# Wv's preparation merged into the block of LN1 and V, with the x rows loaded ahead of Wv and the weight maxima of four tiles put behind their rows

## The reference

```python
# x: (1, 2048, 1024) float32; 16 heads of 64; FFN of 2752 with NF4 weights in blocks of 64
def reference(x, Wq, Wk, Wv, Wo, gate, up, down):      # each FFN weight: codes and scales
    h = layernorm(x)
    q, k, v = rotary(h @ Wq), rotary(h @ Wk), h @ Wv
    attn = softmax(causal(q @ k.T) / 8) @ v
    x = x + layernorm(attn @ Wo)
    h = layernorm(x)
    y = (silu(h @ dequant(gate).T) * (h @ dequant(up).T)) @ dequant(down).T
    return x + layernorm(y)
```

## Time and profile before

| | |
|---|---|
| median of three runs | 3296.17 us |
| the profiled execution | 3296.03 us, span 3294.2 us |
| TensorE matmul busy | 2897.0 us (88%) |
| VectorE busy | 2390.9 us (73%) |
| ScalarE busy | 2022.5 us (61%) |
| GpSimd busy | 121.6 us (4%) |
| TensorE's granted clock, mean | 0.964 of full |
| first projection matmul of V starts | 47.70 us after the span's start |
| first matmul of the Q and K projection | 242.61 us |

### The profile page before, as it was taken

One profiled execution on the slowest core, in us unless ns is written; L12 is line 12 of the kernel. 1 busy time (PEld: TensorE's weight loads), 2 busy tenths in 40 slices (PEclk: granted clock), 3 DMA queues, 4 the chain that ended last, 5 costly groups with the idle time before them and its releaser, 6 DMA issues. The chain is left out here.

```text
span 3294.2 us, 58839 instructions
## 1 busy us (share of the span) xinstructions
PE 2897.0 (88%) x17856; PEld 1547.4 (47%) x17856; DVE 2390.9 (73%) x4289; ACT 2022.5 (61%) x4003; POOL 121.6 (4%) x397
## 2 busy tenths in 40 slices
PE   4989999688888888985883699999999999999996
PEld 2534444466666666663441244444444444444442
DVE  6535555688888888884556787787777777777767
ACT  1114443688888888882214767676676676676742
POOL 0000000000000000000002000000000000000002
PEclk9999999899999999997996899999999999999998
DMA  4322222201010101102112111111111111111124
GB/s 164 116 77 58 76 76 64 72 22 40 22 41 22 40 22 35 27 5 86 64 70 69 53 52 49 50 52 52 46 52 49 50 52 45 53 46 52 52 71 153
DMA packets 77773, 188.88 MB, mean 57 GB/s; under 512 B 12304, under 2 KB 12688, under 8 KB 77200
## 3 DMA queue, kind: packets, MB, share of 16 engines
q1 hardware_dynamic: 77456, 185.13, 17.7%
HBM read 151.52 MB, written 33.55 MB: 56 GB/s over the span
## 5 line engine op out<-in xcount | busy, mean ns | idle before, releaser
L1234 PE MATMUL gp<-region,wgu 128*128 128x512 f16 x4224 | 931.3, 383 | 89.3 <-DVE wgu L1392 89.3
L1271 ACT ACTIVATE line<-code,offsets 128x512 f32<-128x512 f32 x1056 | 697.2, 713 | 111.3 <-DVE below L1370 45.7
L1234 PEld LDWEIGHTS gp<-region,wgu 128*128 128x128 f16 x4224 | 416.0, 99 | 600.9 <-issue 110.9
L786 ACT ACTIVATE probs<-logits,nbias,coef 128x512 f32<-128x512 f32 (+3 forms) x640 | 461.0, 720 | 100.4 <-POOL nbias L719 86.4
L1247 PE MATMUL yp<-wd,inter 128*128 128x512 f16 x2112 | 463.9, 380 | 24.5 <-DVE wd L1392 17.4
L835 DVE SCALAR_TENSOR_TENSOR pt_pair<-tp,pt_pair 128x512 f16<-128x512 f32 (+3 forms) x640 | 385.8, 603 | 76.2 <-ACT pt_pair L795 72.4
L736 PE MATMUL logits<-k_sb,q_sb 128*128 128x512 f16 (+3 forms) x1280 | 347.3, 354 | 104.6 <-ACT probs L786 61.2
L819 DVE TENSOR_REDUCE mx<-logits 128x1 f32<-128x512 f32 (+3 forms) x640 | 383.9, 600 | 33.7 <-PE logits L736 33.1
L795 ACT ACTIVATE pt_pair<-tp 128x512 f16<-128x512 f32 (+3 forms) x640 | 343.4, 537 | 25.2 <-PE tp L749 21.0
L749 PE MATMUL tp<-ident,probs 128*128 128x128 f32 x2176 | 349.2, 276 | 4.3 <-DVE pt_pair L835 2.7
L548 PE MATMUL pq<-region,wt_pair 128*128 128x512 f16 x1536 | 333.4, 380 | 14.9 <-DVE wt_pair L599 14.9
(11 more groups left out here) (107 smaller groups left out, 2823.0 us busy)
## 6 DMA issues: line engine op xcount, KB each, us to landing
qk_pairs<-r_pair SPq DMA_DIRECT2D x128, 128.0 KB, 2.1
k_sb<-qk_pairs SPq DMA_DIRECT2D x64, 256.0 KB, 5.4
cst<-in_gate_codes SPq DMA_DIRECT2D x44, 256.0 KB, 2.6
sst<-in_gate_scales SPq DMA_DIRECT2D x88, 128.0 KB, 2.9
cst<-in_up_codes SPq DMA_DIRECT2D x44, 256.0 KB, 2.7
sst<-in_up_scales SPq DMA_DIRECT2D x88, 128.0 KB, 3.1
cst<-in_down_codes SPq DMA_DIRECT2D x44, 256.0 KB, 2.7
sst<-in_down_scales SPq DMA_DIRECT2D x88, 128.0 KB, 3.0
```

Of the source, the lines that this page charges most:

```text
L786: a.activation(probs[:, g0 % P_RING, 0:w * P], sp_[:, g0 % S_RING, 0:w * P], ACT.Exp, bias=nbias[:, m:m + 1], scale=col(coef, 0), accum_ou ...
L1234: mm = pe.matmul(gp[:, e % 2, m, :], wgu[:, par, m, a, col0:col0 + P], xnT[:, b, k, tok], start=(k == 0 and a == b), stop=(k == KT - 1 and ...
L1271: a.activation(line[:, k % 4, :], code7[:, :], ACT.Identity, scale=slope, bias=offsets[:, k:k + 1]).then_inc(s_L.sem, 1)
```

## The change

- The first block is gone. Its work stands in the block of LN1 and V, in the same lists as the x tiles.
- SyncE's order: x tile 0, four Wv tiles, x tile 1, four Wv tiles, weights of tiles 0 and 1, `flat`, x tiles 2 and 3, weights of tiles 2 and 3; from tile 4 on rows and weights in turn as before.
- VectorE's order: rows of tile 0, four Wv maxima, rows of tile 1 and low half of tile 0, four Wv maxima, all-reduce and factor of Wv alone, eight low halves of Wv, tiles 2 and 3 of rows with `lo` and `v_lo` as in the loop but without weight maxima; then in one piece the weight maxima of tiles 0 to 3, the clearing of `sums` and the maxima of `flat`; then the loop, with weight maxima inside `rows` again.
- The first projection waits for each low half of Wv by itself (`s_wvlo`) in its first 24 matmuls.
- GpSimd: constants, inverse roots of tiles 0 and 1, the all-reduce of Wv's maximum, then the other roots.
- The last all-reduce and the factors at the block's end take seven columns for three, and three coefficient products moved there from the first block.

```diff
@@ -188,7 +188,7 @@
         mask_f32 = sb("mask_f32", [P, P], F32, c04)
         mask_bf = sb("mask_bf", [P, P], BF16, c04)
         sums = sb("sums", [P, ST, HEADS, SC], F32, c04)
-        Q_, K_, O_, V_, G_, U_, D_ = range(7)
+        Q_, K_, O_, G_, U_, D_, V_ = range(7)
 
         def col(t, n):
             return t[:, n:n + 1]
@@ -217,79 +217,6 @@
 
         c01 = ctx.enter_context(ExitStack())
         wv_pair = sb("wv_pair", [P, 2, KT, E], F16, c01)
-        ...
-        c0.close()
-
         def layernorm_stats(v, chain, parts, st, variance):
 
             for n, part in enumerate(parts):
@@ -309,6 +236,8 @@
 
 
         c1 = ctx.enter_context(ExitStack())
+        flat = sb("flat", [P, 3, I * E // BLOCK // P], F32, c1)
+        vmax = sb("vmax", [P, KT], F32, c1)
         xt = sb("xt", [P, 2, E], F32, c1)
         ht = sb("ht", [P, 2, E], F32, c1)
         wst = sb("wst", [P, 2, 3, CH], F32, c1)
@@ -318,6 +247,15 @@
         vp = ps("vp", [P, 2, 2, CH], F32, c1)
         d_x = loads("d_x", 2)
         d_ws = loads("d_ws", 2, 3)
+        d_wv = loads("d_wv", KT)
+        d_flat = loads("d_flat", 1, 3)
...
         s_c1 = sem("s_c1")
         s_h = signal("s_h", 2)
         s_wm = signal("s_wm", 2)
@@ -341,17 +279,34 @@
 
             @block.sync
             def _(sp):
-                def step(i, it, u):
+                def rows(i, u):
                     sp.wait_ge(s_h.sem, s_h.room(i))
                     sp.dma_start(xt[:, u, :], x_tiles[bass.ds(i, 1)].rearrange("a p e -> p (a e)")
                                  ).then_inc(d_x.sems[u], 16)
+
+                def weights(i, u):
                     sp.wait_ge(s_wm.sem, s_wm.room(i))
                     for m in range(3):
                         sp.dma_start(wst[:, u, m, :], w_parts[m][bass.ds(i, 1)].rearrange("a p e -> p (a e)")
                                      ).then_inc(d_ws.sems[u], 16)
-                with sp.Fori(0, ST // 2) as it:
+                wv_v = wv.rearrange("(k p) n -> p k n", p=P)
+                rows(0, 0)
+                for k in range(KT):
+                    sp.dma_start(wv_f32[:, k, :], wv_v[:, k, :]).then_inc(d_wv.sems[k], 16)
+                    if k == 3:
+                        rows(1, 1)
+                for u in range(2):
+                    weights(u, u)
+                for m in range(3):
+                    sp.dma_start(flat[:, m, :], scales_flat[m]).then_inc(d_flat.sems[0], 16)
+                for u in range(2):
+                    rows(2 + u, u)
+                for u in range(2):
+                    weights(2 + u, u)
+                with sp.Fori(2, ST // 2) as it:
                     for u in range(2):
-                        step(it * 2 + u, it, u)
+                        rows(it * 2 + u, u)
+                        weights(it * 2 + u, u)
 
             @block.tensor
             def _(pe):
@@ -364,19 +319,25 @@
                         mm = pe.transpose(tp[:, u, k, :], ht[:, u, k * P:(k + 1) * P], ident[:, :])
                     mm.then_inc(s_T1.sem, 1)
 
-                def project(i, u):
+                def project(i, u, first=False):
                     pe.wait_ge(s_tlo.sem, s_tlo.done(i))
                     pe.wait_ge(s_vlo.sem, s_vlo.room(i))
                     for n in range(2):
                         for k in range(KT):
+                            if first and n == 0:
+                                pe.wait_ge(s_wvlo.sem, s_wvlo.done(k))
                             for a, b in ((0, 0), (0, 1), (1, 0)):
                                 mm = pe.matmul(vp[:, u, n, :], hT[:, a, k, bass.ds(i * P, P)],
                                                wv_pair[:, b, k, n * CH:(n + 1) * CH],
                                                start=(k == 0 and a == b), stop=(k == KT - 1 and a == 1))
                     mm.then_inc(s_V.sem, 1)
 
+                pe.wait_ge(s_id.sem, s_id.done(4))
                 transposes(0, 0)
-                with pe.Fori(0, ST // 2 - 1) as it:
+                for u in range(2):
+                    transposes(u + 1, 1 - u)
+                    project(u, u, u == 0)
+                with pe.Fori(1, ST // 2 - 1) as it:
                     for u in range(2):
                         transposes(it * 2 + u + 1, 1 - u)
                         project(it * 2 + u, u)
@@ -397,6 +358,10 @@
                                  scale=QKV_DOWN).then_inc(s_vhi.sem, 1)
 
                 hi(0, 0)
+                a.wait_ge(s_facv.sem, s_facv.done(0))
+                for k in range(KT):
+                    a.activation(wv_pair[:, 0, k, :], wv_f32[:, k, :], ACT.Copy,
+                                 scale=col(wfac, V_)).then_inc(s_wvhi.sem, 1)
                 with a.Fori(0, ST // 2 - 1) as it:
                     for u in range(2):
                         hi(it * 2 + u + 1, 1 - u)
@@ -410,16 +375,20 @@
                 for s in (s_h, s_wm, s_tlo, s_vlo):
                     v.sem_inc(s.sem, s.credit)
 
-                def rows(i, it, u):
-
-                    chain = Count(s_c1, i * CHAIN1)
-                    v.wait_ge(d_x.sems[u], d_x.done(it))
-                    layernorm_stats(v, chain, (xt[:, u, 0:CH], xt[:, u, CH:E]), st1[:, u, :], s_var1)
+                def weights(i, it, u):
                     v.wait_ge(d_ws.sems[u], d_ws.done(it))
                     for m in range(3):
                         mx = v.tensor_reduce(wmax[:, m, bass.ds(i, 1)], wst[:, u, m, :], AX_X, ALU.max,
                                              apply_absolute_value=True)
                     mx.then_inc(s_wm.sem, 1)
+
+                def rows(i, it, u, between=None):
+
+                    chain = Count(s_c1, i * CHAIN1)
+                    v.wait_ge(d_x.sems[u], d_x.done(it))
+                    layernorm_stats(v, chain, (xt[:, u, 0:CH], xt[:, u, CH:E]), st1[:, u, :], s_var1)
+                    if between:
+                        between(i, it, u)
                     v.wait_ge(s_root1.sem, s_root1.done(i))
                     v.tensor_scalar(st1[:, u, 14:15], st1[:, u, 14:15], H_SCALE, None, ALU.mult).then_inc(chain.sem, chain.one())
                     v.wait_ge(chain.sem, chain.at)
@@ -440,12 +409,47 @@
                         in1=v_rows[:, bass.ds(i, 1), :, 0:D].rearrange("p a h d -> p (a h) d"),
                         op0=ALU.mult, op1=ALU.subtract).then_inc(s_vlo.sem, 1)
 
+                first = Count(s_c0)
+                v.wait_ge(s_id.sem, s_id.done(5))
+                v.tensor_copy(ident_bf[:, :], ident[:, :]).then_inc(first.sem, first.one())
+                v.tensor_copy(mask_bf[:, :], mask_f32[:, :]).then_inc(first.sem, first.one())
                 rows(0, 0, 0)
+                for k in range(4):
+                    v.wait_ge(d_wv.sems[k], d_wv.done(0))
+                    v.tensor_reduce(col(vmax, k), wv_f32[:, k, :], AX_X, ALU.max,
+                                    apply_absolute_value=True).then_inc(first.sem, first.one())
                 rows(1, 0, 1)
                 lo(0, 0)
-                with v.Fori(0, ST // 2 - 1) as it:
+                for k in range(4, KT):
+                    v.wait_ge(d_wv.sems[k], d_wv.done(0))
+                    v.tensor_reduce(col(vmax, k), wv_f32[:, k, :], AX_X, ALU.max,
+                                    apply_absolute_value=True).then_inc(first.sem, first.one())
+                v.wait_ge(first.sem, first.at)
+                v.tensor_reduce(col(absmax, V_), vmax[:, :], AX_X, ALU.max).then_inc(s_maxv.sem, 1)
+                v.wait_ge(s_allv.sem, s_allv.done(0))
+                powers(v, first, V_, V_ + 1)
+                v.sem_inc(s_facv.sem, 1)
+                for k in range(KT):
+                    v.wait_ge(s_wvhi.sem, s_wvhi.done(k))
+                    v.scalar_tensor_tensor(out=wv_pair[:, 1, k, :], in0=wv_f32[:, k, :], scalar=col(wfac, V_),
+                                           in1=wv_pair[:, 0, k, :], op0=ALU.mult,
+                                           op1=ALU.subtract).then_inc(s_wvlo.sem, 1)
+                for u in range(2):
+                    rows(u + 2, 1, u)
+                    lo(u + 1, 1 - u)
+                    v_lo(u, u)
+                for it in range(2):
                     for u in range(2):
-                        rows(it * 2 + u + 2, it + 1, u)
+                        weights(it * 2 + u, it, u)
+                v.memset(sums[:, :, :, :], 0.0).then_inc(first.sem, first.one())
+                v.wait_ge(d_flat.sems[0], d_flat.done(0))
+                for m, c in enumerate((G_, U_, D_)):
+                    v.tensor_reduce(col(absmax, c), flat[:, m, :], AX_X, ALU.max,
+                                    apply_absolute_value=True).then_inc(first.sem, first.one())
+                v.wait_ge(first.sem, first.at)
+                with v.Fori(1, ST // 2 - 1) as it:
+                    for u in range(2):
+                        rows(it * 2 + u + 2, it + 1, u, weights)
                         lo(it * 2 + u + 1, 1 - u)
```

(38 more changed lines are left out.)

67 lines of the change are left out of this document (removed).

## The result

The kernel after the change took 3306.64 us (median of 7 runs, 3304.66 to 3309.0), the kernel before 3296.07 beside it: ratio 1.0034, with a 95% interval of 1.0022 to 1.0045. It is slower by about 11 us; the forecast was 3289.4, faster by 6.7. The profiled span grew from 3294.2 to 3303.5.

What follows compares the result with a forecast made beforehand. It took the opening to be latency until project(0) can start, then bound by TensorE. Of 18.2 us gained there 7.6 stay after the new stall; 7.6 - 0.93 = 6.7 off, giving 3289.4, range 3285 to 3295.5.

Steps and rivals of the forecast that it cites:

- What bounds the kernel: Opening: latency until project(0) can start, then TensorE at 11.23 us a tile; later stages untouched, moving as a block.
- Added wait on GpSimd: Ahead of the all-reduce: configuration change of 8.2 us after root 1 at 15.8, all-reduce starting at 24.0, 0.65 late.
- project(0): First V projection: ends at 41.95 instead of 60.11, 18.2 us earlier, assuming the full clock by then.
- the rival of the half clock: In project(0): half-filled TensorE stays at the lower clock, costing up to 5.2 us, total 3294.6; chance 13%.
- Given back: Tiles after project(0): postponed VectorE work stalls TensorE 7.6 us, slow restart, project(3) ends at 86.2; 7.6 of 18.2 stay.
- The rival without a stall: Behind the first projections: VectorE's 11.8 us of postponed work vanish in spare time, 17.3 stay, total 3279; chance 3%.
- The end of the block: Ahead of the Q projection: three coefficient products moved behind the last all-reduce add 0.93 us, all on the path.
- The other side: Rival on GpSimd ahead of the all-reduce: configuration change of 16.1 us, factor 7.9 later, total 3297.3; chance 6%.
- a mishap behind the listed ones: Whole kernel: slower by over 0.2% only through something beyond the listed rivals; chance 0.04.
- five rivals: Half clock, surviving clock or shorter stall, no stall, long configuration change, merged block without effect on time; together 37%.

Runs made afterwards that it cites:

- Experiments 1 and 2: TensorE's attention loop moved within its 256-instruction code block: changed kernel put back at slot 3, 3290.26 us; kernel before placed at slot 227, 3316.3 us.
- experiment 9: Changed kernel with the inverse roots of x tiles 0 and 1 taken off GpSimd (VectorE adds eps and takes a reciprocal): 3303.37 us, ratio 1.0018.
- experiment 8: Changed kernel with the postponed maxima spread over the loop and between V's last low halves, TensorE's program unchanged: 3291.26 us, ratio 0.9992.
- slot 196: Kernel before with TensorE's attention loop at slot 196 of its 256-instruction block, 60 instructions left behind the branch: 3299.52 us, ratio 1.0009.
- slot 128: Kernel before with TensorE's attention loop at slot 128 of its 256-instruction block, 128 instructions left: 3296.06 us, ratio 1.0002.

## Why the prediction was wrong

- **What bounds the kernel: the step that failed** is "Later stages start behind this one and are not touched, so they move as a block". They were not touched in their text, but moved in their blocks of instructions, and the attention stage grew from 882.2 to 897.1. Experiments 1 and 2 show it from both sides: the place alone costs the kernel after 16.4 us (3306.64 to 3290.26) and the kernel before 21 (3295.19 to 3316.3). The prediction gave everything behind the opening a cost of nothing; the branches of 3.7 us stood in the trace of before, and I had not looked at any.
- **Added wait on GpSimd: right mechanism, mis-sized.** Root 1 ended at 15.0 (15.8 forecast), the change took 9.9 us and not 8.2, and the maximum was there 1.3 us earlier than forecast. So the all-reduce was late by 2.9 (24.91 against some 22.0), not by 0.65; experiment 9 bears this out (4.0 earlier, 1.1 of it by the maximum). The factor came at 26.1 (25.2).
- **project(0)** ended at 43.04 (41.95), with its last 27 matmuls at the full clock (6.00 us); the rival of the half clock falls.
- **Given back: right place, mis-sized.** A stall of 9.46 was forecast as 7.6. Both late weight tiles were waited for (2.40 and 1.57), where I had the second landed; the rows of tile 4 began at 70.46, not 67.6. The restart was as forecast (1.97 and 12.36). Left of the merge: 4.7 at project(3), not 7.6. The rival without a stall, at 3%, was no rival of this order; experiment 8 shows what it is worth when the order is changed.
- **The end of the block: right.** The wait in front of Q is 15.77, 0.9 more.
- Sum for what the change touches: 3.8 instead of 6.7. With the loop at slot 3 the changed kernel takes 3290.26, within 0.9 of the forecast, but that is in part luck: the opening gave 2.9 less than forecast, and its attention stage happens to be 3.7 under that of before.
- **The other side.** My slower rival was the library change at 16.1 us; it took 9.9. Only 4% was left for a mishap behind the listed ones, and it was one of those. The forecast and its five rivals already add up to 100%, so these 4% are taken out of the 6% of the library change.

Open: why the second block is fetched only behind the first; why the moment of entry into the loop is worth 4 to 6 us of the stage; where between 60 and 29 instructions the cost sets in; and how the places of ScalarE's and VectorE's loops matter (they were not moved). The 3.9 us of slot 196 over before are not clear of noise; in its profile 2.2 of them are in the attention stage (884.4).

## What to carry to other kernels

An edit that adds or removes instructions ahead of a loop moves the loop's head within its block of instructions, and may cost more there than it gains; look at the branches (their duration, the gap behind them, the granted clock) before holding a later stage for untouched. When a stage gets slower turn by turn and its waits end on "issue", put the loop back in its old place first: it is one line, and tells at once. Work that is postponed should go in portions where its engine is idle each turn, not in one piece ahead of what the next engine waits for.

## What the runs showed of the hardware that I had not expected

- A branch back of the attention loop takes TensorE 3.4 to 3.9 us (4.4 and 4.8 in two turns of slot 128), most of it an idle TensorE; hinted, 0.34 to 0.48. The turn gets 3.2 us shorter with the hint on TensorE, ScalarE and VectorE, and 0.3 with TensorE alone.
- The block behind the target's is asked for 4.1 to 4.9 us after the branch and at work 6.3 to 7.4 us after it. With 128 instructions left to run until then, nothing is lost; with 60, up to 0.88 us of gap; with 29 or 18, 0.5 to 2.4 us, and TensorE at 0.50 of its clock for mostly 6.8 us around it, where 3.4 us at this level cost 1.5.
- GpSimd's change from tensor_tensor to the all-reduce takes 9.9 us (14.98 to 24.91, its input there from 21.9 on), the opposite one 8.2. By the Trainium skill, GPSIMD Engine Reference, section 2.1 Instruction dispatch, such a first call pays about 6 us; the trace agrees in kind, and is longer both times.
